# Two attention passes with score tiles (head of pair, query) x (graph, key), unswapped values and 64x64 output products; all loops written out

## The reference

```python
def L2(x, adj):                      # pass 2
    q = (x @ Wq.T).reshape(B, N, 12, 32)
    k = (x @ Wk.T).reshape(B, N, 12, 32)
    v = (x @ Wv.T + bv).reshape(B, N, 12, 32)
    a = einsum('bnhd,bmhd->bhnm', q, k) * 384 ** -0.5 + adj[:, None]
    pad_mask = all(a == 0, axis=-1)  # such a row gives zeroes
    a = nan_to_num(softmax(where(pad_mask[..., None], -inf, a)))
    return einsum('bhnm,bmhd->bnhd', a, v).reshape(B, N, 384) @ Wo.T + bo

def L3(x, adj):                      # pass 3
    q, k, v = (split_heads(x @ W + b) for W, b in ((Wq, bq), (Wk, bk), (Wv, bv)))
    s = einsum('bhqd,bhkd->bhqk', q, k) / sqrt(32) + beta * adj[:, None]
    p = softmax(where(adj[:, None] > 0, s, -9e15))
    return einsum('bhqk,bhkd->bhqd', p, v)

x = layernorm(x + L(x, adj))         # for each of the four layers
```

## Time and profile before

| | us |
|---|---|
| median of 3 runs | 3243.24 |
| lowest, highest | 3242.81, 3244.91 |
| profiled execution, first to last instruction | 3245.9 |
| pass 0 and pass 1, TensorE's first to last instruction | 9 to 937, 966 to 1854 |
| pass 2 and pass 3, the same | 1882 to 2619, 2634 to 3234 |

### The profile page before, as it was taken

How to read it: one execution, slowest core, us unless ns; L and a number is a source line. 1 busy time by engine, 2 the same in 40 slices (tenths; PEclk the granted TensorE clock), 3 DMA queues, 4 the chain that set the end, 5 groups by cost and what they waited for, 6 DMA issues and landing times. The chain is left out here.

```text
span 3245.9 us, 63935 instructions
## 1 busy us (share of the span) xinstructions
PE 2997.6 (92%) x22272; PEld 2535.5 (78%) x22272; DVE 2343.3 (72%) x5327; ACT 1178.1 (36%) x2689; POOL 1478.6 (46%) x1239
## 2 busy tenths in 40 slices
PE   7999899999859999999999879999999969999998
PEld 6887788888748878877878658888888858888886
DVE  5877777777755766566567668888888867777777
ACT  2344334433422222222222234344443324444443
POOL 6766666666646555555555523222222112333323
PEclk8999999999979999999999989999999989999999
DMA  3101101110111110011011021111110011111111
GB/s 113 44 19 38 36 23 36 42 36 23 33 58 51 43 47 27 21 47 37 19 39 46 11 79 32 33 42 42 42 42 21 32 45 34 53 53 42 42 51 42
DMA packets 132014, 131.15 MB, mean 40 GB/s; under 512 B 56032, under 2 KB 131808, under 8 KB 131808
## 3 DMA queue, kind: packets, MB, share of 16 engines
q1 hardware_dynamic: 131808, 128.55, 12.9%
HBM read 78.19 MB, written 50.33 MB: 40 GB/s over the span
## 5 line engine op out<-in xcount | busy, mean ns | idle before, releaser
L1380 POOL TENSOR_TENSOR l_prob<-l_prob,l_mx 128x512 f32<-128x512 f32 x192 | 200.4, 1044 | 776.5 <-DVE l_mx L1217 776.5
L691 POOL TENSOR_TENSOR l_hlo<-l_hf,l_hhi 128x576 fp32r<-128x576 f32 (+1 forms) x192 | 259.7, 1378 | 405.4 <-DVE l_hhi L488 293.3
L501 DVE TENSOR_TENSOR l_val<-l_ring,l_vec 64x384 f32<-64x384 f32 x512 | 284.4, 555 | 140.6 <-PE l_ring L292 124.2
L292 PE MATMUL l_ring<-whi,l_hhi 128*128 128x384 f32 x1152 | 270.8, 344 | 8.6 <-DVE l_val L501 8.5
L292 PE MATMUL l_ring<-whi,l_hlo 128*128 128x384 f32 x1152 | 264.7, 338 | 8.5 <-POOL l_hlo L691 8.5
L292 PE MATMUL l_ring<-wlo,l_hhi 128*128 128x384 f32 x1152 | 263.5, 338 | 0.0
L305 PE MATMUL l_ctx<-l_val,l_dt 128*64 128x385 f32 (+1 forms) x768 | 214.4, 568 | 46.8 <-DVE l_dt L645 35.1
L971 PE MATMUL l_ring<-l_hhi,whi 128*128 128x512 f32 x576 | 235.4, 409 | 8.2 <-DVE l_hlo L1197 7.9
L456 ACT ACTIVATE l_mt<-l_ring 128x512 f32<-128x512 f32 x192 | 114.9, 598 | 324.8 <-PE l_ring L356 324.8
L971 PE MATMUL l_ring<-l_hhi,wlo 128*128 128x512 f32 x576 | 229.4, 398 | 0.0
L971 PE MATMUL l_ring<-l_hlo,whi 128*128 128x512 f32 x576 | 229.4, 398 | 0.0
(11 more groups left out here) (186 smaller groups left out, 7259.8 us busy)
## 6 DMA issues: line engine op xcount, KB each, us to landing
x<-l_za SPq DMA_DIRECT2D x24, 768.0 KB, 3.9
x<-l_zb SPq DMA_DIRECT2D x24, 768.0 KB, 3.6
l_xa<-x SPq DMA_DIRECT2D x32, 384.0 KB, 3.1
l_xb<-x SPq DMA_DIRECT2D x32, 384.0 KB, 3.2
l_xa<-x SPq DMA_DIRECT2D x16, 768.0 KB, 5.3
l_xb<-x SPq DMA_DIRECT2D x16, 768.0 KB, 6.0
out<-l_za SPq DMA_DIRECT2D x8, 768.0 KB, 3.6
out<-l_zb SPq DMA_DIRECT2D x8, 768.0 KB, 3.6
```

The source lines that it names most:

```text
L292: mm = nc.tensor.matmul(bank(k)[:, 0:D], hh[:, c, first:first + P], ww[:, c, :], start=(j == 0), stop=(j == len(terms) - 1))
L501: ins = nc.vector.tensor_tensor(out, bank(k)[half, 0:D], bias[half, :], ALU.add)
L691: nc.gpsimd.tensor_tensor(hlo[:, c, :], hf[:, c, :], hhi[:, c, :], ALU.subtract).then_inc(lo_done, 1)
L1380: nc.gpsimd.tensor_tensor(row, row, mx[:, c, ts, :].rearrange("p t h -> p (t h)").unsqueeze(2) .broadcast_to([P, 2 * HP, S]), ALU.subtract)\
```

## The change

in_turns writes out all eight turns, for all engines and passes, so that every count is a constant and no engine jumps back.

In heads_pass the scores are laid out anew. A unit is a pair of heads, not half a chunk of tiles. Its tile is (head of pair, query) x (graph, key): 128 partitions by 8 graphs of 64 keys. The weights are qpair, 64 rows (two heads of 32 features) by 128 columns (query block of the one head, of the other, with zeroes for the other's features), the moving side 64 columns of keys, now stored plainly. Products alternate the lower and the upper 64 rows (units of a chunk, u = 0 and 1), into two banks. The queries come out of PSUM by two operations, scaled by the column of_pair of ones and zeroes, the keys by one, all on ScalarE; keys_out is gone from VectorE. The mask is loaded for all graphs in both halves (adj_by_graph).

Values stay in the partitions where they are made: one operation a tile, and vside, swap's product and ScalarE's copies (L999, L1241, L1131) are gone. Transposed probabilities are (graph of tile, key) x (head of pair, query), and outputs makes 24 products a tile of 64 rows by 64 weights with 33 columns, graph b of the tile in the b half of rows and of columns, into bank ot[b]; so each tile uses both banks, and outputs(t) waits for divide(t-1). divide has two operations of 64 partitions in place of each of 128. In pass 2 a row of zeroes is known by a flag, `empty`, made per unit and added to the maximum, and the sum is held at 0.5 or above before its reciprocal.

The order in a slot changes with it: the third chunk of scores stands ahead of values of tiles 2 and 3, and of the transpositions of x; the probabilities' transposition waits for all six units; queries_keys 2 to 5 stand one by one between the output tiles instead of ahead of them. The memset of keys and the zeroes of val are gone, and the second count of `cleared` comes behind the wait for the vectors.

```diff
 def in_turns(eng, turns, body):
-    body(0, turns == 1)
-    if turns > 2:
-        with eng.Fori(1, turns - 1) as i:
-            body(i, False)
-    if turns > 1:
-        body(turns - 1, True)
+    for i in range(turns):
+        body(i, i == turns - 1)
...
-        q = sb("q", [P, KC, R])
-        keys = sb("keys", [P, KC, GRAPHS, HP, S])
-        vside = sb("vside", [P, 2, PAIRS, HD])
-        val = sb("val", [P, GRAPHS, PAIRS, 2, HO])
-        prob = sb("prob", [P, KC, T, HP, S])
+        qpair = sb("qpair", [P, KC, GRAPHS, 2, S])
+        keys = sb("keys", [P, KC, R])
+        val = sb("val", [P, T, H, HO])
+        prob = sb("prob", [P, UNITS, GRAPHS, S])
...
             def chunk_scores(n, c):
                 pe.wait_ge(s_evac, UNITS * n + 2 * c)
                 for g in range(GRAPHS):
-                    p0, t = S * (g % 2), g // 2
-                    mm = nc.tensor.matmul(scores[t // 2][p0:p0 + S, (t % 2) * HP * S:(t % 2 + 1) * HP * S],
-                                          q[:, c, g * S:(g + 1) * S], keys[:, c, g, :, :].rearrange("p h j -> p (h j)"),
-                                          start=True, stop=True)
+                    for u in range(2):
+                        two = slice(S * u, S * u + S)
+                        mm = nc.tensor.matmul(scores[u][:, g * S:(g + 1) * S],
+                                              qpair[two, c, g, :, :].rearrange("p h i -> p (h i)"),
+                                              keys[two, c, g * S:(g + 1) * S], start=True, stop=True)
                 mm.then_inc(s_done, 1)
...
             def outputs(n, t):
                 pe.wait_ge(pt_evac, 2 * (T * n + t + 1))
-                pe.wait_ge(n_done, T * n + max(t - 1, 0))
-                for b in range(2):
-                    rows = slice(S * b, S * b + S)
-                    for m in range(PAIRS):
-                        mm = nc.tensor.matmul(ot[t % 2][rows, 2 * m * HO:2 * (m + 1) * HO], probt[t % 2][:, m, rows],
-                                              val[:, 2 * t + b, m, :, :].rearrange("p h f -> p (h f)"),
+                pe.wait_ge(v_evac, T * n + t + 1)
+                pe.wait_ge(n_done, T * n + t)
+                for h in range(H):
+                    for b in range(2):
+                        rows = slice(S * b, S * b + S)
+                        mm = nc.tensor.matmul(ot[b][rows, h * HO:(h + 1) * HO],
+                                              probt[t % 2][rows, h // 2, h % 2 * S:h % 2 * S + S], val[rows, t, h, :],
                                               start=True, stop=True)
                 mm.then_inc(o_done, 1)
...
-                values(n, range(0, 2))
+                values(n, [0])
                 chunk_scores(n, 1)
-                for t in range(2):
-                    values(n, [t + 2])
-                    sides(n, [t])
+                values(n, [1])
+                chunk_scores(n, 2)
+                values(n, range(2, T))
                 if not last:
                     rows_transposed(n + 1, i + a, 1 - a, range(0, 2))
-                chunk_scores(n, 2)
-                sides(n, range(2, 4))
...
-                    queries_keys(n + 1, range(2 * KC - 1))
+                    queries_keys(n + 1, range(0, 2))
                 probs_transposed(n, 0)
-                if not last:
-                    queries_keys(n + 1, [2 * KC - 1])
                 for t in range(1, T):
+                    if not last:
+                        queries_keys(n + 1, [t + 1])
                     probs_transposed(n, t)
                     outputs(n, t - 1)
+                if not last:
+                    queries_keys(n + 1, [5])
                 outputs(n, T - 1)
...
+            def scores_out(n, a, c):
+
+                for k in range(2 * c, 2 * c + 2):
+                    dve.wait_ge(s_done, KC * n + c + 1)
+                    dve.wait_ge(pt_done, 2 * T * n)
+                    nc.vector.scalar_tensor_tensor(prob[:, k, :, :].rearrange("p g j -> p (g j)"), scores[k % 2][:, :], scale,
+                                                   adjp[a][:, :, :].rearrange("p g j -> p (g j)"), ALU.mult, ALU.add)\
+                        .then_inc(s_evac, 1)
+
+            def maxima(n, c):
+
+                for k in range(2 * c, 2 * c + 2):
                     dve.wait_ge(s_evac, UNITS * n + k + 1)
                     if project:
-                        nc.vector.tensor_reduce(amx[:, c, ts, :].rearrange("p t h -> p (t h)"), row, AX.X, ALU.max,
-                                                apply_absolute_value=True)
-                    nc.vector.tensor_reduce(mx[:, c, ts, :].rearrange("p t h -> p (t h)"), row, AX.X, ALU.max)\
-                        .then_inc(mx_done, 1)
+                        found = mx_step.mark(nc.vector.tensor_reduce(amx[:, k, :], prob[:, k, :, :], AX.X, ALU.max,
+                                                                     apply_absolute_value=True))
+                        nc.vector.tensor_reduce(mx[:, k, :], prob[:, k, :, :], AX.X, ALU.max)
+                        dve.wait_ge(mx_steps, found)
+                        mx_step.after(nc.vector.tensor_scalar(empty[:, k, :], amx[:, k, :], 0.0, NEVER, ALU.is_equal, ALU.mult))
+                        nc.vector.tensor_tensor(mx[:, k, :], mx[:, k, :], empty[:, k, :], ALU.add).then_inc(mx_done, 1)
...
+                for b in range(2):
+                    rows = slice(S * b, S * b + S)
+                    den = by_head(ot[b][rows, 0:H * HO])[:, :, HD]
                     if project:
+                        ins = nc.vector.tensor_scalar(rec[rows, t, :], den, 0.5, None, ALU.max)
                     else:
+                        ins = nc.vector.reciprocal(rec[rows, t, :], den)
+                steps.after(ins)
+                if project:
+                    steps.after(nc.vector.reciprocal(rec[:, t, :], rec[:, t, :]))
```

More of the change, by code:

```diff
@@ L891, in slots @@
             in_turns(eng, iters, turn)
-        def key_parts(k, heads):
-            return [(part, keys[part, k - KC, :, h, :], ring[k % 2][part, :].rearrange("p (g j) -> p g j", j=S))
-                    for h in heads for part in [slice(HD * h, HD * h + HD)]]
         @block.sync
@@ L1314, in final_apply @@
                 fsteps.end()
-            nc.vector.memset(keys[:, :, :, :, :], 0.0)
-            nc.vector.memset(val[:, :, :, :, :], 0.0).then_inc(cleared, 1)
+            for r in range(HP):
+                for p in range(2):
+                    nc.vector.memset(of_pair[HD * r:HD * r + HD, p:p + 1], float(r % 2 == p))
+            nc.vector.memset(val[:, :, :, HD:HO], 1.0).then_inc(cleared, 1)
             dve.wait_ge(cleared, 1)
-            for p in range(2):
-                ins = nc.vector.memset(val[S * p:S * p + S, :, :, p, HD:HO], 1.0)
@@ L1321, in _ @@
-            ins.then_inc(cleared, 1)
-            dve.wait_ge(cleared, 2)
+            dve.wait_ge(vec_in, vecs)
+            if project:
+                nc.vector.memset(small[:, 3, :], 0.0).then_inc(cleared, 1)
+            else:
+                for p in range(2):
+                    ins = nc.vector.tensor_scalar(qbias[:, p, :], colvec[:, 0, :], of_pair[:, p:p + 1], None, ALU.mult)
+                ins.then_inc(cleared, 1)
             low_parts(0, range(KC))
-            dve.wait_ge(vec_in, vecs)
@@ L1339, in body @@
+                values_out(n, [0])
+                scores_out(n, a, 1)
+                maxima(n, 1)
+                values_out(n, [1])
+                scores_out(n, a, 2)
+                maxima(n, 2)
+                values_out(n, range(2, T))
                 if not last:
                     low_parts(n + 1, range(0, 2))
-                if not last and not project:
-                    low_parts(n + 1, [2])
-                maxima(n, a, [4])
                 if project and not first:
                     results_out(n - 1, 1 - a, range(0, 2))
-                if not last and project:
+                if not last:
```

246 lines of the change are left out of this document (97 added, 149 removed).

## The result

| | before, us | after, us |
|---|---|---|
| median of 4 runs each | 3243.02 | 3275.08 |
| lowest, highest | 3240.09, 3244.91 | 3272.65, 3277.28 |
| span of the profiled execution | 3245.9 | 3270.9 |
| pass 0, TensorE's first to last instruction | 928.4 | 949.1 |
| pass 1 | 887.3 | 850.5 |

The changed kernel is slower: the ratio is 1.0099, with a 95% interval from 1.0086 to 1.0111. The passes account for +20.7, -36.8, +32.3 and +8.4 us, together +24.6 of the 25.0 us between the spans.

What follows compares the result with a forecast made beforehand. TensorE was taken as the bound, busy 96 to 99%, with VectorE second in pass 2. Terms -33 + 25 + 24 + 10 - 9 - 6 = +11 on 3245.9 gave 3257, less 2.7 for timed runs 3254 us; range 3208 to 3302.

Steps and rivals of the forecast that it cites:

- the likeliest case: The forecast itself, 3254 us for the whole kernel, given chance 0.4 and its own range 3240 to 3272.
- pass 3: New arrangement, 15 slots: sides gone 1.9 us, waits added 1.3, so -0.6 a slot, -9 us, without the start.
- Pass 1: Loops written out: TensorE's standstill and slow first products at five jumps back go, -33 us.
- Pass 0: Loops written out: GpSimd's vdiag addition starts ahead of VectorE's ediag in slot 1, six turns at 4.24, +25 us.
- Pass 2: New arrangement: swap exchange goes, two waits for VectorE come, +1.6 us a slot for 15 slots, +24; clock and start separate.
- The outputs: Output products in passes 2 and 3: 48 records x 31 ns a tile against 24 x 57, called unchanged.
- The clock: TensorE's clock drops behind the new 2.2 us wait in pass 2: 0.7 us a slot, +10 us (0 to 25).
- The starts: Starts of passes 2 and 3: memsets go and the last keys come out by one operation, -6 us.
- VectorE did not keep winning in pass 0: Rival: VectorE's ediag still starts ahead of GpSimd in pass 0's middle turns, no +25, 3229 us; chance 0.2.
- Its chain in pass 2 did not hide: Rival: VectorE's chain in pass 2 runs 3.5 us a slot shorter, neither wait appears, 3190 us (half: 3222); chance 0.12.
- The row halves do run side by side: Rival claimed they don't: scores 3.4 us a chunk, 3360 us, or 3495 with outputs serial too; chance 0.1.
- GpSimd did not hold up the small operations: Rival: GpSimd delays VectorE's empty-row flag and addition in pass 2, up to 1.0 us on three units, 3300; chance 0.15.

Runs made afterwards that it cites:

- b_flat: The kernel before with all turns written out and nothing else changed: 3229.75 us, ratio 0.9961.
- a_wait: The changed kernel with GpSimd waiting for VectorE's ediag before its addition to vdiag, in slots 0 and 1 of pass 0: 3225.95 us, ratio 0.9949.
- a_loop0: The changed kernel with the six middle turns of pass 0 looped again: 3256.07 us, ratio to before 1.0045.
- a_noempty: The changed kernel without VectorE's flag of empty rows and its addition to the maximum: 3247.42 us, ratio to before 1.0015.
- a_order: The changed kernel with the third chunk of scores moved behind the values of tile 2: 3300.36 us, ratio to before 1.0169.
- a_noalt: The changed kernel with scores ordered by row half and outputs by graph, so neighbours no longer alternate array parts: 3782.85 us, ratio 1.1653.
- b_alt: The kernel before with its output products alternating between the two graphs of a tile (column halves): 3199.17 us, ratio 0.9871.

## Why the prediction came out as it did

The forecast was 3254 us and the time is 3275.08, slower as forecast, inside the range of 3208 to 3302 but above the likeliest case's own 3240 to 3272. Against the profiled span the sum was +11 and came to +25. Passes 0, 1 and 2 together are 7 us below their terms; pass 3 was -12 with its share of the start and is +8.4, a miss of 20.

**Pass 1** was -33 and is -36.8. The mechanism was right (b_flat shows it alone); a written-out middle turn takes 633.12 / 6 = 105.5 us, where I had taken the last turn's 106.0, whose stretch runs on past its last product.

**Pass 0** was +25 and is +20.7. The race was lost in all turns, at 0.01 us as in the earlier trace rows: 6 x 4.3 = 26, less some 0.8 in each of the six turns that other slots gained. What I did not see: slot 0 pays for the same race before the change as well, some 3.7 us in a looped turn (31.2 before, 27.5 in a_wait). a_wait shows that the choice of 25 against 0 was one on the order of two starts, which an explicit wait settles.

**Pass 2** was +31 with the start (24 + 10 - 3) and is +32.3, but not by those parts. Its start gave -5.0, the 15 slots +28.1, the last slot +9.1. That the pass came out within 1.3 us is luck: in a_loop0 and a_wait the same arrangement cost 36.4 and 39.1.

| in a slot of pass 2, us | predicted | measured |
|---|---|---|
| wait for VectorE, third chunk | 1.35 | 0.84 |
| wait for VectorE, first result | 2.2 | 1.90 |
| exchange through swap, with its wait | -2.0 | -1.9 |
| outputs, four tiles | 0 | +0.9 |
| scores, three chunks | 0 | +0.1 |
| all else | 0 | -0.1 |
| slot, from 44.8 | 46.35 | 46.55 |

The waits stand where they were forecast, and a_noempty and a_order show what they are. They are shorter by 0.8 than the sum of ten operations made them. That error was covered by the next.

**The outputs are the term that was mis-sized**, and with it pass 3, -9 a pass against +8.9 for the same 15 slots. I set 48 x 31 ns against 24 x 57 ns and called them unchanged. The 57 ns is the mean busy time of a record, and the old outputs overlapped at every change of half (starts 3 to 6 ns apart there), so that four tiles took 5.1 us from start to start, not 5.5; the new ones took 6.1 (pairs 58 ns apart, 24 of them, and 0.12 to begin). That is +1.0 a slot in pass 3. The others there were swap -1.9 with its wait (as predicted), the wait for low parts +0.9 (I had 1.3), scores +0.2 and queries and keys, broken up into single products, +0.4 (I had nothing for either); together +0.6, where I had -0.6. The groups of both kernels show records and busy time only:

```profile
L995 PE MATMUL l_ot<-l_val,l_probt 64*64 64x33 f32 x6144 | 208.2, 223 | 12.1 <-DVE l_o L1219 7.4 <-DVE l_zb L1219 4.7
```

208.2 us stand against the 173.8 of L1031 in the earlier trace rows: 34 us more, over 32 slots 1.1 a slot.

**The clock** was +10 in 15 slots and cost 1.6 there, in one slot. It fell in five, but in four of them behind the wait at the third chunk, where the wait at the first result took it up (see a_order). The second slot of the pass took 1.2 us more than the next ones and another 0.4, both at full clock, by waits. Larger was a cost for which I had no term, in **the last slot** of pass 2, +9.1, and of pass 3, +2.6. outputs(t) now waits for the division of tile t - 1 and not of t - 2. I had that covered by the queries and keys between the tiles, and the last slot has none. The step that failed there is this cover, which I costed for a slot in the middle and not for the last. The traces show the waits; no run was made without them.

**The starts** were -6 and are -8. That of pass 3 is -3.0 and holds in every run with the new arrangement (-2.0 to -3.3). That of pass 2 is -5.0, but the same code gave -3.4 in a_loop0 and +0.8 in a_wait, so its part of the agreement is luck.

**The rivals.** VectorE did not keep winning in pass 0. Its chain in pass 2 did not hide. The row halves do run side by side: at 3.88 us a chunk and 2.78 a tile, a_noalt is the world of that rival, for which I had 3495 us; it takes 3783, with the clock that I had left out. GpSimd did not hold up the small operations, 0.16 and 0.17 us in all 96.

The Trainium skill (Runtime: NRT & Kernel Launch, Instruction fetch mechanics) says that a taken jump can stall on the fetch of its target and that kernels therefore prefer full unrolling. Pass 1 agrees, -36.2 us in b_flat; by itself it would not give the +20.4 us of pass 0, as the trace of before had said. The Trainium skill (SBUF — State Buffer, SBUF: two separate sides) says that whichever of the two starts first holds the shared port pair for its whole instruction. The ediag rows agree: 3.2 or 3.47 us when GpSimd starts just ahead, 0.43 when it waits.

## What to carry to other kernels

Before an arrangement is changed for the sake of small products, look whether the old ones stand in an order in which neighbours can run side by side: three swapped lines gave 42 us, where the rebuilt passes cost 39 to 45. When loops are written out, look for pairs of VectorE and GpSimd that become ready within tenths of a microsecond, and order them by a wait. Price products by the distance from start to start of a whole tile, and price every new wait a second time for the last slot, where the work that covers it is missing. When the clock falls in a slot, look whether a wait for another engine comes behind the slow stretch: if so, the drop may cost nothing.

## What the runs showed of the hardware

Delaying GpSimd by 0.7 to 1.0 us saved 55 us in a pass, since a VectorE operation of 0.42 us had been waiting for a GpSimd one of 3.2 in 15 slots, where it took 3.2 to 3.5 us.

TensorE's clock fell to its lower level with no idle time ahead of it, while small products ran one after the other (a window of 10 us, busy for all of it, at 0.56). And slots with the same work and the same waits ran with and without a drop: behind a wait of 1.99 us 46.55 or 48.11 us, nine times in 15 the longer. A drop behind a wait of 0.84 us cost nothing, since the next wait, for VectorE, shrank from 1.90 to 0.31.

Products of different column halves that write the same PSUM bank overlap as well as those that write two banks: pairs of outputs start 6 ns apart in both b_alt and the kernel after, and the pairs follow each other at 58 ns.
